# Transposes on TensorE read through fp32r tiles, in a four-stage transformer kernel

## The chip, the cores and the metric

The kernel runs on one core of a Trainium2 chip. The metric is device time in microseconds (us) of one execution; it was run three times. The parts of a core that matter here are TensorE (PE in the profile; its weight loads are listed apart as PEld), VectorE (DVE), ScalarE (ACT), GpSimd (POOL) and SyncE (SP), which issues most of the DMAs. Each engine works its own list of instructions in order and waits on semaphores for the others.

## The reference

Four layers with a residual and a layer norm behind each, on x of 4 x 256 rows of 512 float32 values:

```python
x = L0_attn_hidden_size
x = _layernorm(x + _L0_attn_ref(x, ...))   # 32 heads, latent q and kv, softmax over 256 keys
x = _layernorm(x + _L0_ffn_ref(x, ...))    # silu(x gate.T) * (x up.T), then down, inner width 1376
x = _layernorm(x + _L1_attn_ref(x, ...))   # 32 heads, causal within 128 rows
x = _layernorm(x + _L1_ffn_ref(x, ...))    # dense layer plus 8 gated low-rank experts
```

Both attentions are the usual one:

```python
scores = jnp.einsum('bhqd,bhkd->bhqk', q, k) * scale
probs = jax.nn.softmax(scores, axis=-1)
attn = jnp.einsum('bhqk,bhkd->bqhd', probs, v)
```

## The kernel before

**Numbers.** Nearly every product is made of three matmuls in the reduced 32-bit type fp32r: each operand is split into a high and a low part of that type, and `matmul3` (L101 to L103) adds high x high, low x high and high x low in PSUM. The matmuls whose operands are plain float32 are few: clearing two banks at the start (L354, L361), merging two weights per head (L881), the sum of the first attention's output (L972), and all transposes.

**Transposes.** TensorE contracts over the partitions, so what comes out of one step with rows on the partitions has to be turned before it can be contracted over columns. `pe.transpose(out, in_, identity)` turns one block of 128x128: the block is loaded as weights and the identity is streamed through (one LDWEIGHTS and one MATMUL in the profile, operands `g_ident` and the block). The result lies in PSUM; ACT writes its high part and DVE the low part. There are 1008 blocks:

- L916 (`turn` in the first attention): the probabilities `h_pr`, 4 blocks in a row, 128 times (32 heads x 4 batches).
- L2235 (`turn` in the second attention): `c_pr`, 3 blocks in a row, 128 times.
- L2674 (last layer): the normed rows `e_x`, 4 blocks, 8 times; L2695: the weighted experts `e_wh`, one block, 8 times.
- L1125 and L1153 (class `Norm`): 64 blocks of the rows `g_res`; L406: 8 blocks of `p_kvraw`.
- L1012: a single column of 128 maxima (`mag1`), not counted above.

**First attention (about 26 to 355 us).** The loop runs over heads h and, in a head, over four rounds b, one per batch. TensorE's round is: scores of round s+1 (two `matmul3`), then a query or a projection, then `turn` of round s-1, then the values of round s-3 (L930, four matmuls), then in some rounds the merge of the next head's weights (L881). DVE's round is: inverse of the exp sums (L755), maxima (L750), then by round a part of the merge (L726, which waits for L881), query low part (L744) or output low part (L764), then the low part of the turned probabilities (L759). ACT does the exps (L657) and high parts (L651, L663, L668), POOL the division of the probabilities (L604), which waits for L755 and is waited for by `turn`. Each engine's order is fixed in the code.

**Second attention (about 520 to 1325 us).** A planner lists pieces of PE work of 16 head pairs in one order: scores, turn, values, and between them the projections of the next pair (`c_bx`, `c_by`, `c_bv`). Scores of a step are followed at once by `turn` of an earlier step (L2235).

**Names.** `Kit.sb` reserves a tile and keeps it; `Kit.under` reserves a tile and gives its place back at once, so the next tile reserved has the same addresses. `ident` is made on POOL in `constants` (L263 to L266); `g["ident"]` is what all transposes stream.

Of the kernel before, what the change touches and what calls it, by code (L numbers as in the profile page):

```python
# [34 lines left out]
ALU = mybir.AluOpType  # L35
# [34 lines left out]
    return ap.bitcast(F32)  # L70


def need(eng, sem, value):

    if isinstance(value, int) and value <= 0:
        return
    eng.wait_ge(sem, value)
# [28 lines left out]
class Kit:  # L106
# [5 lines left out]
    def sb(self, name, shape, dt=F32):  # L112
        return self.ctx.enter_context(self.nc.sbuf_tensor(f"{self.tag}_{name}", shape, dt))

    def under(self, name, shape, dt=F32):

        with self.nc.sbuf_tensor(f"{self.tag}_{name}", shape, dt) as tile:
            return tile
# [8 lines left out]
def build(nc, io):  # L127
    with ExitStack() as ctx:
        k = Kit(nc, ctx, "g")
        g = {  # L130
            "res": k.sb("res", [P, NT, HID]),
            "bvs": k.sb("bvs", [P, 1]),
            "xT": (k.sb("xT_hi", [P, KC, T], F32R), k.sb("xT_lo", [P, KC, T], F32R)),
            "ident": k.sb("ident", [P, P]),
            "o_last": k.under("o_last", [P, 2, T], F32R),
            "y": k.sb("y", [P, 4, HID]),
            "wo": k.sb("wo", [P, HID]),
            "mag": k.sb("mag", [P, NH]),
            "mag1": k.sb("mag1", [P, 1]),
            "largest": k.sb("largest", [1, 1], I32),  # L140
            "tick": k.sem("tick"),
            "ln": {n: k.sem(n) for n in ("st", "mv", "add", "rs", "xn", "t", "hi", "lo")},
            "m": {"st": k.sb("st", [P, NT, 6]), "mv": k.sb("mv", [P, NT, 2]), "rs": k.sb("rs", [P, NT]),
                  "mh": k.sb("mh", [P, 4])},
        }
# [56 lines left out]
class Latents0:  # L202
# [7 lines left out]
    def __init__(self, k, io, g, first, down):  # L210
        self.io, self.g, self.first = io, g, first
        self.whi, self.wlo = down
        self.qa = (k.sb("qa_hi", [P, T], F32R), k.sb("qa_lo", [P, T], F32R))
        self.qb = k.sb("qb", [P, T], F32R)
        self.cs = k.sb("cs", [P, NT, P], F32R)
        k.sb("gap0", [P, 16])
        self.kv = (k.sb("kv_hi", [P, T], F32R), k.sb("kv_lo", [P, T], F32R))
        self.bias = k.sb("bias", [P, 16])[:, 0:3]
        self.bv = k.sb("bv", [P, NH])
        self.bo = k.sb("bo", [P, HID])  # L220

        with ExitStack() as ctx:
            t = Kit(k.nc, ctx, "p")
            self.xraw = t.sb("xraw", [P, KC, T])
            self.wraw = t.sb("wraw", [P, KC, 3 * P])
            t.sb("gap", [P, KC, 3 * P])
            self.zero = t.sb("zero", [P, P])
            self.kvraw = t.sb("kvraw", [P, T])
# [29 lines left out]
        sp.wait_ge(self.s_xlo, 2 * KC)  # L258

    def constants(self, pool):  # L260
        ident = self.g["ident"]
        pool.memset(self.zero[:, :], 0.0).then_inc(self.s_id, 1)
        pool.memset(ident[:, :], 0.0).then_inc(self.s_id, 1)  # L263
        pool.wait_ge(self.s_id, 2)
        pool.affine_select(out=ident[:, :], in_=ident[:, :], compare_op=ALU.not_equal, fill=1.0, base=0,
                           pattern=[[-1, P]], channel_multiplier=1).then_inc(self.s_id, 1)  # L266
        pool.memset(self.g["m"]["mh"][:, :], -0.5).then_inc(self.s_pre, 1)
        pool.wait_ge(self.s_xlo, 2 * KC)

# [127 lines left out]
            self.product(pe, i, c)  # L397

    def turn(self, pe, n):
        pe.wait_ge(self.s_id, 3)  # L400
        pe.wait_ge(self.s_raw, n + 1)
        if n:
            pe.wait_ge(self.s_lo, 5)
        for j in range(4):
            a = (4 * n + j) * P
            mm = pe.transpose(self.turn_banks[n][:, j * P:(j + 1) * P], self.kvraw[:, a:a + P], self.g["ident"][:, :])  # L406
        mm.then_inc(self.s_tr, 1)


def attention0_heads(nc, k, io, g, lat, acc, first, tail, norm, ffn, after, attn1, layer1):  # L410
# [13 lines left out]
    with ExitStack() as ctx:  # L424
# [10 lines left out]
        o = [(t.sb(f"o{i}_hi", [P, HALF], F32R), t.sb(f"o{i}_mix", [P, HALF], F32R)) for i in range(2)]  # L435

        gb = t.sb("gb", [P, 16])[:, 0:1]
        pr = [t.sb(f"pr{i}", [P, 2, S]) for i in range(NB)]
        pt = [(t.sb(f"pt{i}_hi", [P, 2, S], F32R), t.sb(f"pt{i}_lo", [P, 2, S], F32R)) for i in range(NB)]
        nmax = [t.sb(f"nmax{i}", [P, 2]) for i in range(NB)]  # L440
        rsum = [t.sb(f"rsum{i}", [P, 2]) for i in range(NB)]
# [83 lines left out]
        with nc.Block() as block:  # L525
# [197 lines left out]
            def _(dve):  # L723
# [44 lines left out]
                def round_(h, b):  # L768
# [22 lines left out]
                        probs(s - 2, (b - 2) % 4)  # L791
                    if isinstance(s, int) and s == NS - 1:
                        dve.wait_ge(s_mag, NH)
                        dve.tensor_reduce(g["mag1"][:, :], g["mag"][:, :], AX, ALU.max).then_inc(s_mag1, 1)
# [79 lines left out]
            def _(pe):  # L874
# [132 lines left out]
                def last_values(d):  # L1007
                    if d == 0:
                        values(NS - 3, NPAIR - 2, 1, 1)
                        pe.wait_ge(s_exp, NS - 1)  # L1010
                        pe.wait_ge(s_mag1, 1)
                        pe.transpose(bs[0][0:1, 0:P], g["mag1"][:, :], ident[:, :]).then_inc(s_magT, 1)  # L1012
                        turn(NS - 1, 3)
                        out(1)
                    elif d == 1:
# [52 lines left out]
class Norm:  # L1068
# [3 lines left out]

    def __init__(self, g, nth):
        self.res, self.xT, self.ident, self.m, self.s = g["res"], g["xT"], g["ident"], g["m"], g["ln"]
        self.tiles = nth * NT
        self.counts = ((1, 2, 3, 3), (4, 4, 6, 8), (9, 9, 10, 10))[nth]

# [42 lines left out]
    def turn(self, pe, j, banks):  # L1120
        pe.wait_ge(self.s["xn"], self.tiles + j + 1)
        need(pe, self.s["lo"], self.tiles + j + 1 - len(banks))
        for c in range(KC):
            cols = slice(c * P, (c + 1) * P)
            i = pe.transpose(banks[j % len(banks)][:, cols], self.res[:, j, cols], self.ident[:, :])  # L1125
        i.then_inc(self.s["t"], 1)

    def view(self, j, banks):
# [17 lines left out]
    def turn_pair(self, pe, a, banks):  # L1146

        pe.wait_ge(self.s["xn"], self.tiles + a + 2)
        for k_half, bank in enumerate(banks):
            for c in range(2):  # L1150
                for i in range(2):
                    k = (2 * k_half + c) * P
                    m = pe.transpose(bank[:, c * S + i * P:c * S + (i + 1) * P], self.res[:, a + i, k:k + P],  # L1153
                                     self.ident[:, :])
            m.then_inc(self.s["t"], 1)

    def view_pair(self, bank):
# [372 lines left out]
class Attention1:  # L1530
# [128 lines left out]
    def programs(self, k, before, after, ffn0, end):  # L1659
# [14 lines left out]
        oT_all = k.sb("oT", [P, 2, 2, T], F32R)  # L1674
        oT = (oT_all[:, 0, :, :], oT_all[:, 1, :, :])

        pr = [k.sb(f"pr{i}", [P, 3 * P]) for i in range(2)]
# [467 lines left out]
        def tensor(pe):  # L2145
# [245 lines left out]
class FFN1:  # L2391
# [4 lines left out]
    def __init__(self, k, io, g, raw, norm):  # L2396
        res, ident, m = g["res"], g["ident"], g["m"]
        ws = [ffn1_part(raw, c)[1:] for c in range(KC)]
        bm = ffn1_part(raw, KC)[1:]
        x = [k.sb(f"x{i}", [P, HID]) for i in range(2)]  # L2400
# [4 lines left out]
        wh = k.sb("wh", [P, E, R])  # L2405
# [264 lines left out]
        def turn(pe, t, u):  # L2670
            pe.wait_ge(s_x, t + 1)
            need(pe, s_xlo, t)
            for c in range(KC):
                i = pe.transpose(bx[:, c * P:(c + 1) * P], x[u][:, c * P:(c + 1) * P], ident[:, :])  # L2674
            i.then_inc(s_tx, 1)

        def first(pe):
# [4 lines left out]
        def tensor(pe):  # L2682
# [9 lines left out]
            def turn_weighted(t):  # L2692
                pe.wait_ge(s_wh, 2 * t + 2)
                need(pe, s_whl, t)
                pe.transpose(bw[:, 0:P], wh[:, :, :].rearrange("p e r -> p (e r)"), ident[:, :]).then_inc(s_tw, 1)  # L2695

            def combined_last():
                out, hi, lo = br[1][:, :], whT[0][:, :], whT[1][:, :]
# [122 lines left out]
```

## Time and profile before

| | |
|---|---|
| median of 3 runs | 1427.53 us (1427.49 to 1427.69) |
| profiled execution, its own time | 1427.42 us |
| span of the profiled execution | 1425.5 us |
| PE busy | 1412.4 us (99%) |
| PEld busy | 1251.5 us (88%) |
| DVE, ACT, POOL busy | 1018.5, 890.7, 773.3 us |
| chain that ended last | PE 94% of the span |

The span runs from the first to the last instruction; 1.9 us of the execution's own time lie around it. "Busy" counts a matmul from its start to its modelled end, and matmuls overlap: what a matmul costs is read from the distance between the starts of neighbours, not from its duration. The profile writes f32 for float32 and for fp32r reads of TensorE alike; which one it is stands in the code.

### The profile page before, as it was taken

To read this page: it belongs to the slowest core of one execution; us is meant where nothing else is said; L and a number is where in the kernel's file an instruction comes from. 1 tells how busy PE (TensorE), PEld (TensorE's weight loads), DVE (VectorE), ACT (ScalarE), POOL (GpSimd) and SP (SyncE) were. 2 spreads that over 40 slices of the span, in tenths; PEclk is the share of its full clock that TensorE was granted. 3 is DMA by queue.
4 is the path that set the end of the run, shared out by engine and by line. 5 is a ranking of instruction groups with operands and counts; after the bars stand their busy time and mean duration, and the time that the engine had idled before them with its cause. 6 is when DMAs were issued, how large, how long until landed. Compare 5 with 4: busy or idle time off the path is not lost.

```text
span 1425.5 us, 30206 instructions
## 1 busy us (share of the span) xinstructions
PE 1412.4 (99%) x8769; PEld 1251.5 (88%) x8769; DVE 1018.5 (71%) x2528; ACT 890.7 (62%) x2445; POOL 773.3 (54%) x827
## 2 busy tenths in 40 slices
PE   9999999999999999999999999999999999999998
PEld 7899999998788888889889889889889889889887
DVE  5999999998868875665665665565565665665776
ACT  5888888888555576555555555556556556556711
POOL 3555555555040367765765665665665665665521
PEclk9999999999999999999999999999999999999999
DMA  5533333322445301111001001001101001000201
GB/s 195 167 95 94 95 94 95 93 66 50 127 140 161 98 30 60 31 30 59 29 29 59 29 29 59 29 29 59 29 29 59 29 29 59 29 29 29 82 16 46
DMA packets 56155, 92.60 MB, mean 65 GB/s; under 512 B 6064, under 2 KB 27312, under 8 KB 56112
## 3 DMA queue, kind: packets, MB, share of 16 engines
q1 hardware_dynamic: 55968, 91.93, 21.5%
q8 instruction: 23, 0.38, 0.1%
q14 instruction: 20, 0.16, 0.0%
q10 hardware_dynamic: 144, 0.13, 0.0%
HBM read 81.82 MB, written 2.10 MB: 59 GB/s over the span
## 4 chain that ended last, share of the span: by engine, by line
PE 94%; DVE 2%; ACT 1%; issue 1%; POOL 1%; DMA 0%; SPq 0%; POOLq 0%; DVEq 0%; ACTq 0%
PE c_bv L101 7%; PE c_bv L102 7%; PE c_bv L103 7%; PE c_bx L101 4%; PE c_bx L103 4%; PE c_bx L102 4%; PE h_bo L930 4%; PE h_bt L916 4%; PE c_by L103 4%; PE c_by L102 4%; PE c_by L101 4%; PE c_bt L2235 3%; PE a_acc L1432 3%; PE h_bo L1432 3%; PE h_bs L101 2%; PE h_bs L103 2%
## 5 line engine op out<-in xcount | busy, mean ns | idle before, releaser
L604 POOL TENSOR_TENSOR h_pr<-h_pr,h_rinv 128x512 f32<-128x512 f32 x128 | 133.2, 1041 | 138.3 <-DVE h_rinv L755 136.0
L1763 POOL TENSOR_TENSOR c_qk<-g_y,c_qk 128x512 fp32r<-128x512 f32 x96 | 124.1, 1293 | 154.1 <-ACT c_qk L1875 147.4
L1614 POOL TENSOR_TENSOR b_sw_lo<-b_slots,b_sw_hi 128x512 fp32r<-128x512 f32 (+1 forms) x128 | 148.1, 1157 | 10.2
L1612 POOL CAST b_sw_hi<-b_slots 128x512 fp32r<-128x512 f32 (+1 forms) x128 | 72.8, 569 | 142.8 <-DMA b_slots<-in_w_qk 123.1
L102 PE MATMUL c_bv<-b_wv_lo,g_xT_hi 128*128 128x256 f32 x496 | 138.8, 280 | 0.0
L101 PE MATMUL c_bv<-b_wv_hi,g_xT_hi 128*128 128x256 f32 x496 | 138.7, 280 | 0.0
L103 PE MATMUL c_bv<-b_wv_hi,g_xT_lo 128*128 128x256 f32 x496 | 138.6, 279 | 0.0
L1984 DVE TENSOR_TENSOR c_bo<-c_bo,g_wo 128x128 f32<-128x128 f32 x128 | 38.3, 299 | 122.6 <-ACT g_wo L1850 118.3
L1875 ACT ACTIVATE c_qk<-g_y 128x512 fp32r<-128x512 f32 x96 | 60.6, 632 | 99.4 <-DVE g_y L2021 69.3
L657 ACT ACTIVATE h_pr<-h_bs,h_nmax 128x256 f32<-128x256 f32 x256 | 119.0, 478 | 2.5 <-DVE h_nmax L750 2.4
L1840 ACT ACTIVATE c_pr<-c_pr,c_rinv 128x128 f32<-128x128 f32 (+1 forms) x256 | 101.9, 448 | 9.0 <-DVE c_rinv L1974 9.0
L102 PEld LDWEIGHTS c_bv<-b_wv_lo,g_xT_hi 128*128 128x128 f32 x496 | 93.1, 188 | 4.5
L101 PEld LDWEIGHTS c_bv<-b_wv_hi,g_xT_hi 128*128 128x128 f32 x496 | 93.2, 188 | 4.4
L1832 ACT ACTIVATE c_pr<-g_wo,c_nmax 128x128 f32<-128x128 f32 x128 | 51.6, 403 | 69.9 <-DVE c_nmax L1970 66.1
L1594 POOL TENSOR_TENSOR b_slots<-b_slots 128x256 f32<-128x256 f32 x128 | 93.1, 747 | 2.5
L1845 ACT ACTIVATE c_pt<-c_bt 128x384 fp32r<-128x384 f32 x128 | 62.9, 491 | 49.5 <-PE c_bt L2235 47.6
L103 PEld LDWEIGHTS c_bv<-b_wv_hi,g_xT_lo 128*128 128x128 f32 x496 | 93.0, 187 | 0.0
L2002 DVE TENSOR_TENSOR g_res<-c_bv,g_res 128x512 f32<-128x512 f32 x103 | 71.2, 691 | 27.4 <-PE c_bv L103 27.3
L750 DVE TENSOR_REDUCE h_nmax<-h_bs 128x2 f32<-128x512 f32 x128 | 87.5, 683 | 0.0
L759 DVE TENSOR_TENSOR h_pt_lo<-h_bt,h_pt_hi 128x512 fp32r<-128x512 f32 x128 | 87.1, 681 | 0.2
L1850 ACT ACTIVATE g_wo<-c_bo 128x128 f32<-128x128 f32 x128 | 35.4, 276 | 78.5 <-PE c_bo L2247 78.5
L101 PE MATMUL c_bv<-b_wo_hi,c_oT 128*128 128x512 f32 x200 | 82.0, 410 | 0.0
(479 smaller groups left out, 5184.0 us busy)
## 6 DMA issues: line engine op xcount, KB each, us to landing
f_wi<-in_w_ffn SPq DMA_DIRECT2D x66, 256.0 KB, 2.7
b_slots<-in_w_qk SPq DMA_DIRECT2D x64, 256.0 KB, 2.9
a_w<-in_w_head SPq DMA_DIRECT2D x28, 352.0 KB, 2.9
h_part<-in_w_ffn SPq DMA_DIRECT2D x32, 264.0 KB, 2.7
b_raw_v<-in_w_v SPq DMA_DIRECT2D x16, 512.0 KB, 4.5
b_raw_o<-in_w_o SPq DMA_DIRECT2D x16, 512.0 KB, 4.6
h_o_mix<-h_o_hi SPq DMA_DIRECT2D x62, 128.0 KB, 2.2
b_ffn_w<-in_w_ffn SPq DMA_DIRECT2D x4, 576.0 KB, 5.5
```

Of the source, the lines that this page charges most:

```text
L101: pe.matmul(out, w[0], x[0], start=start, stop=False, skip_group_check=True)
L102: pe.matmul(out, w[0], x[1], start=False, stop=False, skip_group_check=True)
L103: return pe.matmul(out, w[1], x[0], start=False, stop=stop, skip_group_check=True)
L604: pool.tensor_tensor(pr[b][:, :, :], pr[b][:, :, :], rinv[b][:, :][:, :, None].to_broadcast([P, 2, S]), ALU.mult)\
L657: m = act.activation(pr[b][:, i, :], bs[b % 2][:, i * S:(i + 1) * S], ACT.Exp, bias=nmax[b][:, i:i + 1], accum_out=rsum[b][:, i:i + 1])
L750: dve.tensor_reduce(nmax[b][:, :], bs[b % 2][:, :].rearrange("p (a n) -> p a n", a=2), AX, ALU.max, negate=True).then_inc(s_max, 1)
L759: dve.tensor_tensor(pt[b][1][:, :, :], bt[b % 2][:, :].rearrange("p (a n) -> p a n", a=2), f32(pt[b][0][:, :, :]), ALU.subtract).then_inc( ...
L1432: m = pe.matmul(out, a, b, start=start and i == 0, stop=stop and i == len(pairs) - 1, skip_group_check=True)
L1594: pool.tensor_tensor(slot(out), slot(a), slot(b), op).then_inc(self.s_comb, 1)
L1614: pool.tensor_tensor(self.sw[1][:, a:b], self.slots[:, a:b], f32(self.sw[0][:, a:b]), ALU.subtract)\
L1763: pool.tensor_tensor(lo, src, f32(hi), ALU.subtract).then_inc(s_sumlo, 1)
L1840: m = act.activation(x[:, cols], x[:, cols], ACT.Identity, scale=rinv[t % 2][:, i:i + 1])
```

## The change

All transposes go through a new helper, and what they read is declared fp32r. A matmul operand's type is that of its tile, so each tile that is turned gets a twin of type fp32r at the same addresses (`turned`): the twin is reserved and given back, and the float32 tile takes its place. The writers of the tile still write float32; `transpose` reads the twin, and its output in PSUM is seen as fp32r. The identity is a tile of type fp32r: POOL makes it in a float32 tile `square` as before and then copies it (one instruction more); the first transposes wait for the fourth increment instead of the third. On PE, DVE, ACT and SP the instructions and their order are the same as before; POOL has the one copy more, at the start.

```diff
+def transpose(pe, out, rows, ident):
+    return pe.transpose(out.bitcast(F32R), rows, ident)
...
+    def turned(self, name, shape):
+        return self.under(name + "_t", shape, F32R), self.sb(name, shape)
...
-            "ident": k.sb("ident", [P, P]),
+            "ident": k.sb("ident", [P, P], F32R),
...
-        pool.memset(ident[:, :], 0.0).then_inc(self.s_id, 1)
+        pool.memset(square[:, :], 0.0).then_inc(self.s_id, 1)
         pool.wait_ge(self.s_id, 2)
-        pool.affine_select(out=ident[:, :], in_=ident[:, :], compare_op=ALU.not_equal, fill=1.0, base=0,
+        pool.affine_select(out=square[:, :], in_=square[:, :], compare_op=ALU.not_equal, fill=1.0, base=0,
                            pattern=[[-1, P]], channel_multiplier=1).then_inc(self.s_id, 1)
+        pool.wait_ge(self.s_id, 3)
+        pool.tensor_copy(self.g["ident"][:, :], square[:, :]).then_inc(self.s_id, 1)
...
-        pe.wait_ge(self.s_id, 3)
+        pe.wait_ge(self.s_id, 4)
...
-        pr = [t.sb(f"pr{i}", [P, 2, S]) for i in range(NB)]
+        pr_t, pr = zip(*(t.turned(f"pr{i}", [P, 2, S]) for i in range(NB)))
...
-                            m = pe.transpose(bt[b % 2][:, kt * S + i * P:kt * S + (i + 1) * P],
-                                             pr[b][:, i, kt * P:(kt + 1) * P], ident[:, :])
+                            m = transpose(pe, bt[b % 2][:, kt * S + i * P:kt * S + (i + 1) * P],
+                                          pr_t[b][:, i, kt * P:(kt + 1) * P], ident[:, :])
...
-                    m = pe.transpose(bt[:, cols], pr[t % 2][:, cols], ident[:, :])
+                    m = transpose(pe, bt[:, cols], pr_t[t % 2][:, cols], ident[:, :])
```

The other calls (L406, L1012, L1125, L1153, L2674, L2695) are changed in the same way.

## Rows read from the trace of the kernel before

**Rows 1.** The page: busy time and instructions; granted TensorE clock in 40 slices.
```profile
PE 1412.4 (99%) x8769; PEld 1251.5 (88%) x8769; DVE 1018.5 (71%) x2528; ACT 890.7 (62%) x2445; POOL 773.3 (54%) x827
...
PEclk9999999999999999999999999999999999999999
```

**Rows 2.** Stretches: length, busy PE, PEld, DVE, ACT, POOL, granted clock, DMA, GB/s.
```profile
60.00:340.00 280.00, 279.61 (x2024) 255.57 (x2024) 261.56 (x576) 232.22 (x685) 151.08 (x195) 1.00 0.33 89
340.00:370.00 30.00, 28.78 (x172) 21.56 (x171) 26.93 (x58) 18.36 (x47) 9.54 (x13) 1.00 0.14 40
...
489.00:520.00 31.00, 30.46 (x187) 26.02 (x186) 27.06 (x54) 17.90 (x30) 14.79 (x17) 1.00 0.01 1
520.00:1000.00 480.00, 478.92 (x2974) 428.87 (x2974) 293.96 (x828) 286.93 (x822) 306.18 (x311) 1.00 0.13 42
```

**Rows 3.** Waits, 60 to 340 us: who for whom, us in total, times, longest.
```profile
DVE h_gm L726 <- PE h_bq L881: 10.7, 25, 0.4
...
PE h_bt L916 <- POOL h_pr L604: 0.4, 2, 0.2
```

**Rows 4.** Groups by shape, PE: busy us, mean ns of one, idle before.
```profile
L916 PE MATMUL h_bt<-g_ident,h_pr 128*128 128x128 f32 x512 | 77.2, 273 | 1.3 <-POOL h_pr L604 1.3
...
L2235 PE MATMUL c_bt<-g_ident,c_pr 128*128 128x128 f32 x384 | 63.0, 273 | 0.4 <-ACT c_pr L1840 0.2
```

**Rows 5.** Groups by shape, weight loads.
```profile
L101 PEld LDWEIGHTS c_bv<-b_wv_hi,g_xT_hi 128*128 128x128 f32 x496 | 93.2, 188 | 4.4
L916 PEld LDWEIGHTS h_bt<-g_ident,h_pr 128*128 128x128 f32 x512 | 60.5, 140 | 16.7 <-issue 4.7 <-POOL h_pr L604 2.7
...
L881 PEld LDWEIGHTS h_bq<-a_w 128*128 128x128 f32 x112 | 14.9, 190 | 0.1
```

**Rows 6.** Timeline, PE, second attention: start, length of the piece, instructions.
```profile
604.15 0.22 PE L2247 MATMUL c_bo<-c_pt,c_v_lo 128*128 128x128 f32 x1
604.21 0.33 PE L2225 MATMUL c_bs<-c_qk 128*128 128x256 f32 x1
...
604.85 0.49 PE L2235 MATMUL c_bt<-g_ident,c_pr 128*128 128x128 f32 x3
...
605.41 0.39 PE L102 MATMUL c_bx<-b_ts,b_sw_hi 128*128 128x512 f32 x1
605.64 0.40 PE L103 MATMUL c_bx<-b_ts,b_sw_lo 128*128 128x512 f32 x1
```

**Rows 7.** Timeline, weight loads, three short windows in the first attention.
```profile
351.74 0.14 PEld L916 LDWEIGHTS h_bt<-g_ident,h_pr 128*128 128x128 f32 x1 [0.94 <-POOL h_pr L604]
...
351.74 0.20 PEld L916 LDWEIGHTS h_bt<-g_ident,h_pr 128*128 128x128 f32 x2 [0.94 <-POOL h_pr L604]
...
153.06 0.19 PEld L930 LDWEIGHTS h_bo<-h_pt_hi,a_cs 128*128 128x128 f32 x1
153.16 0.19 PEld L930 LDWEIGHTS h_bo<-h_pt_lo,a_cs 128*128 128x128 f32 x1
```

**Rows 8.** Timeline, PE: float32 matmuls of 512 columns, one and two.
```profile
352.23 0.59 PE L972 MATMUL a_acc<-g_wo,z_os 128*128 128x512 f32 x1
...
352.23 1.02 PE L972 MATMUL a_acc<-g_wo,z_os 128*128 128x512 f32 x2
```

**Rows 9.** Timeline, one head of the first attention: DVE, POOL, PE.
```profile
152.08 0.29 DVE L726 TENSOR_SCALAR h_gm<-h_bq 128x128 f32<-128x128 f32 x1 [0.43 <-PE h_bq L881]
...
162.29 0.29 DVE L726 TENSOR_SCALAR h_gm<-h_bq 128x128 f32<-128x128 f32 x1 [0.43 <-PE h_bq L881]
...
159.53 1.04 POOL L604 TENSOR_TENSOR h_pr<-h_pr,h_rinv 128x512 f32<-128x512 f32 x1 [0.40 <-DVE h_rinv L755]
...
160.78 0.60 PE L916 MATMUL h_bt<-g_ident,h_pr 128*128 128x128 f32 x4
...
161.34 0.28 PE L930 MATMUL h_bo<-h_pt_lo,a_cs 128*128 128x256 f32 x1
161.46 0.28 PE L930 MATMUL h_bo<-h_pt_hi,a_cs 128*128 128x256 f32 x1
```

More of the change, by code:

```diff
@@ L129, in build @@
         k = Kit(nc, ctx, "g")
+        res_t, res = k.turned("res", [P, NT, HID])
         g = {
-            "res": k.sb("res", [P, NT, HID]),
+            "res": res, "res_t": res_t,
             "bvs": k.sb("bvs", [P, 1]),
             "xT": (k.sb("xT_hi", [P, KC, T], F32R), k.sb("xT_lo", [P, KC, T], F32R)),
-            "ident": k.sb("ident", [P, P]),
+            "ident": k.sb("ident", [P, P], F32R),
             "o_last": k.under("o_last", [P, 2, T], F32R),
@@ L138, in build @@
             "mag": k.sb("mag", [P, NH]),
-            "mag1": k.sb("mag1", [P, 1]),
+            "mag1": k.turned("mag1", [P, 1]),
             "largest": k.sb("largest", [1, 1], I32),
@@ L225, in __init__ @@
             self.wraw = t.sb("wraw", [P, KC, 3 * P])
-            t.sb("gap", [P, KC, 3 * P])
+            self.square = t.sb("square", [P, P])
+            t.sb("gap", [P, (3 * KC - 1) * P])
             self.zero = t.sb("zero", [P, P])
-            self.kvraw = t.sb("kvraw", [P, T])
+            self.kvraw_t, self.kvraw = t.turned("kvraw", [P, T])
         self.s_x, self.s_res, self.s_bv, self.s_pre = (k.sem(n) for n in ("x_in", "res_in", "bv_in", "pre"))
@@ L260, in constants @@
     def constants(self, pool):
-        ident = self.g["ident"]
+        square = self.square
         pool.memset(self.zero[:, :], 0.0).then_inc(self.s_id, 1)
-        pool.memset(ident[:, :], 0.0).then_inc(self.s_id, 1)
+        pool.memset(square[:, :], 0.0).then_inc(self.s_id, 1)
         pool.wait_ge(self.s_id, 2)
-        pool.affine_select(out=ident[:, :], in_=ident[:, :], compare_op=ALU.not_equal, fill=1.0, base=0,
+        pool.affine_select(out=square[:, :], in_=square[:, :], compare_op=ALU.not_equal, fill=1.0, base=0,
                            pattern=[[-1, P]], channel_multiplier=1).then_inc(self.s_id, 1)
+        pool.wait_ge(self.s_id, 3)
+        pool.tensor_copy(self.g["ident"][:, :], square[:, :]).then_inc(self.s_id, 1)
         pool.memset(self.g["m"]["mh"][:, :], -0.5).then_inc(self.s_pre, 1)
@@ L405, in turn @@
             a = (4 * n + j) * P
-            mm = pe.transpose(self.turn_banks[n][:, j * P:(j + 1) * P], self.kvraw[:, a:a + P], self.g["ident"][:, :])
+            mm = transpose(pe, self.turn_banks[n][:, j * P:(j + 1) * P], self.kvraw_t[:, a:a + P],
+                           self.g["ident"][:, :])
         mm.then_inc(self.s_tr, 1)
@@ L793, in round_ @@
                         dve.wait_ge(s_mag, NH)
-                        dve.tensor_reduce(g["mag1"][:, :], g["mag"][:, :], AX, ALU.max).then_inc(s_mag1, 1)
+                        dve.tensor_reduce(g["mag1"][1][:, :], g["mag"][:, :], AX, ALU.max).then_inc(s_mag1, 1)
                     if asked and c == 0:
@@ L1011, in last_values @@
                         pe.wait_ge(s_mag1, 1)
-                        pe.transpose(bs[0][0:1, 0:P], g["mag1"][:, :], ident[:, :]).then_inc(s_magT, 1)
+                        transpose(pe, bs[0][0:1, 0:P], g["mag1"][0][:, :], ident[:, :]).then_inc(s_magT, 1)
                         turn(NS - 1, 3)
@@ L1074, in __init__ @@
         self.res, self.xT, self.ident, self.m, self.s = g["res"], g["xT"], g["ident"], g["m"], g["ln"]
+        self.res_t = g["res_t"]
         self.tiles = nth * NT
@@ L1124, in turn @@
             cols = slice(c * P, (c + 1) * P)
-            i = pe.transpose(banks[j % len(banks)][:, cols], self.res[:, j, cols], self.ident[:, :])
+            i = transpose(pe, banks[j % len(banks)][:, cols], self.res_t[:, j, cols], self.ident[:, :])
         i.then_inc(self.s["t"], 1)
@@ L1152, in turn_pair @@
                     k = (2 * k_half + c) * P
-                    m = pe.transpose(bank[:, c * S + i * P:c * S + (i + 1) * P], self.res[:, a + i, k:k + P],
-                                     self.ident[:, :])
+                    m = transpose(pe, bank[:, c * S + i * P:c * S + (i + 1) * P], self.res_t[:, a + i, k:k + P],
+                                  self.ident[:, :])
             m.then_inc(self.s["t"], 1)
@@ L1675, in programs @@
         oT = (oT_all[:, 0, :, :], oT_all[:, 1, :, :])
-        pr = [k.sb(f"pr{i}", [P, 3 * P]) for i in range(2)]
+        pr_t, pr = zip(*(k.turned(f"pr{i}", [P, 3 * P]) for i in range(2)))
         rinv = [k.sb(f"rinv{i}", [P, 2]) for i in range(2)]
@@ L2399, in __init__ @@
         bm = ffn1_part(raw, KC)[1:]
-        x = [k.sb(f"x{i}", [P, HID]) for i in range(2)]
+        x_t, x = zip(*(k.turned(f"x{i}", [P, HID]) for i in range(2)))
         xb = [k.sb(f"xb{i}", [P, HID]) for i in range(2)]
@@ L2404, in __init__ @@
         prod = k.sb("prod", [P, E * DK])
-        wh = k.sb("wh", [P, E, R])
+        wh_t, wh = k.turned("wh", [P, E, R])
         whT = (k.sb("whT_hi", [P, P], F32R), k.sb("whT_lo", [P, P], F32R))
@@ L2673, in turn @@
             for c in range(KC):
-                i = pe.transpose(bx[:, c * P:(c + 1) * P], x[u][:, c * P:(c + 1) * P], ident[:, :])
+                i = transpose(pe, bx[:, c * P:(c + 1) * P], x_t[u][:, c * P:(c + 1) * P], ident[:, :])
             i.then_inc(s_tx, 1)
@@ L2694, in turn_weighted @@
                 need(pe, s_whl, t)
-                pe.transpose(bw[:, 0:P], wh[:, :, :].rearrange("p e r -> p (e r)"), ident[:, :]).then_inc(s_tw, 1)
+                transpose(pe, bw[:, 0:P], wh_t[:, :, :].rearrange("p e r -> p (e r)"), ident[:, :]).then_inc(s_tw, 1)
             def combined_last():
```

## The prediction

> **What bounds the kernel now.** I read the page first: TensorE is busy 99% of the span, its granted clock stands in the top tenth in all forty slices [rows 1]. So the time is TensorE's list, as long as nothing else is late. Then the table by stretches, to see where that is true. In the second attention DVE is busy 294 of 480 us, ACT 287, POOL 306: every other engine has a third of its time free, and PE is at 479 [rows 2]. In the first attention DVE is busy 262 of 280 us; PE is still at 280, but DVE is just behind it. So a nanosecond saved on PE is worth a nanosecond in the second attention, and in the first only until DVE is the bound. The waits of the first attention say how far that is: DVE waits once per head, 25 times in the stretch, 10.7 us in total, 0.43 us each, for the merge matmuls L881; PE waits 0.4 us in all for POOL [rows 3]. Between two heads lie 162.29 - 152.08 = 10.21 us [rows 9]. DVE therefore has 9.78 us of its own per head.
>
> **What one transpose costs now.** Durations mislead, since matmuls overlap; starts count. In the second attention the three transposes start at 604.85 and the second 512-column matmul behind them at 605.41, which is 0.56 us for three transposes and one such matmul; the next distance, 605.41 to 605.64, is 0.23 for one alone [rows 6]. So three cost 0.33, or 0.11 each. In the first attention, 160.78 to 161.34 is 0.56 for four transposes and one matmul of 256 columns, which alone takes 161.46 - 161.34 = 0.12: again 0.11 each [rows 9].
>
> Two things could set this 0.11. One is streaming: the float32 matmuls L972 with 512 columns start 1.02 - 0.59 = 0.43 us apart [rows 8], fp32r ones of 512 columns 0.23 apart [rows 6]. A float32 operand streams at half the pace, and 128 float32 columns are then 0.43 / 4 = 0.11. The other is the weight load. An ordinary load (L930, fp32r) is followed by the next after 153.16 - 153.06 = 0.10 to 0.11 us. A transpose's load that stands free (PE had waited 0.94 us) is followed by the next after 0.20 - 0.14 = 0.06 us [rows 7]; it is also shorter on average, 140 ns against 188 of the fp32r matmuls and 190 of the float32 ones at L881 [rows 5]. So in a transpose of today the streaming (0.11) is the slow half and the load (0.06) the fast one.
>
> **The change part by part.** The identity becomes fp32r, and fp32r streams 128 columns in 604.21 - 604.15 = 0.06 us [rows 6]. If the load keeps its 0.06, a transpose that is followed by another costs 0.06 instead of 0.11: 0.05 saved. The last of a group saves nothing: the matmul behind it needs an ordinary load of 0.10 to 0.11, which today is hidden behind the last transpose's 0.11 of streaming and would then stick out by what the streaming lost. So a group of n saves (n - 1) x 0.05. The unknown is the load under the new type, since no fp32r transpose runs before: from below 0.06 (today's transposes), from above 0.11 (today's fp32r loads of ordinary matmuls, in which case the load alone sets 0.11 and nothing is saved). I take 0.06, because ordinary loads are equally long for float32 and fp32r, 190 and 188 ns, and only the transposes' are short at 140 [rows 5]: the rows point to the transposing and not to the type. Both ends are kept for the range.
>
> The Trainium skill ("TensorE: Matmul & The Clock Gate", section "LDWEIGHTS (loading the stationary operand)") speaks against the change: a load takes the number of columns over 1.2 GHz, 107 ns for 128, whatever is loaded. The free-standing load of today's transposes, 0.06 apart [rows 7], does not agree with it, the ordinary loads do; by the rule alone the sum below would be zero.
>
> - Second attention, 384 transposes [rows 4] in 128 groups of three: 128 x 2 x 0.05 = 12.8 us. All on the path, by [rows 2]. Bounds 0 and 14.
> - First attention, 512 transposes [rows 4] in 128 groups of four: PE's list shrinks by 128 x 3 x 0.05 = 19.2 us, 0.60 per head, to 9.61 us. That is less than DVE's own 9.78, so the whole of it can't come. What DVE waits for is L881, which stands behind the transposes of the same round. Those become 0.15 shorter. They can also start a little earlier: POOL has finished their input at 159.53 + 1.04 = 160.57, PE comes to them at 160.78 [rows 9]; PE will be early after the change and needs the load of 0.06 and the signal from POOL. Without any time for the signal it would start at 160.63, which is 0.15 earlier; with a slow one, nothing is gained. I take the middle, 0.08. DVE's wait falls by 0.15 + 0.08 = 0.23 per head and 0.20 stay. What is late next is POOL's division, and behind it DVE's own order; PE gets idle time of about 0.60 - 0.23 = 0.37 us per head before L916. Over 32 heads: 7.4 us. Bounds: 0.15 x 32 = 4.8 when PE can't start earlier; 0.43 x 32 = 13.8 when the whole wait goes.
> - Last layer, 32 transposes (the kernel's text has their number) in 8 groups of four: 8 x 3 x 0.05 = 1.2 us. The single blocks (L2695) save nothing.
> - The norms' 64 and the 8 of the first keys: 18 groups of four, of which many stand in pairs, so about 60 x 0.05 = 3.0 us of PE. They lie in stretches where DVE is busy 27 of 30 and 27 of 31 us [rows 2]; I count half, 1.5.
> - POOL's copy of the identity is one instruction in the first three microseconds; the first transposes come after 15 us. Nothing, and at most its own some tenths if POOL's list there were late.
> - ACT and DVE read the same PSUM bytes with the same instructions: nothing.
>
> Sum: 12.8 + 7.4 + 1.2 + 1.5 = 22.9 us. The profiled execution took 1427.42 us (span 1425.5 and 1.9 around it), 0.1 below the median of the runs. 1427.4 - 22.9 = 1404.5; I say 1404.
>
> **The rivals.**
> 1. *The new type brings the ordinary load.* The transposes' load becomes 0.11 (or the streaming stays at half pace because all 32 bits have to pass, which comes to the same). For it: every fp32r matmul in the trace has a load of 0.10 to 0.11; that the page's rule says so too is told above. Against it: the short load of today's transposes is of float32, whose ordinary load is as long as fp32r's [rows 5]. Time: 1427.5, within 0.2%.
> 2. *The first attention gives nothing.* The pace is 0.06, but DVE's wait only moves: what PE no longer spends on L916 it spends waiting for POOL, and DVE waits on something else in its round. For it: DVE is busy 93% there [rows 2]. Against it: L881 is directly behind the shortened group. Time: 1427.4 - 15.5 = 1412.
> 3. *Slower: an ordinary load in front of an unchanged stream.* Loads of 0.11 while the streaming stays 0.11. Within a group the two overlap, but the first load of a group that comes late, right after its wait, is not covered, and it is 0.05 longer than today. This decides where PE comes to a group with less than 0.11 of streaming before it: if in all 128 groups of the first attention, 6.4 us, 1434 us. Against it: matmuls of 256 or 512 columns (0.12 and 0.23) stand in front of the groups and would hide it.
>
> **How the numbers follow.** The forecast has 0.54, rival 1 0.26, rival 2 0.12, rival 3 0.08. The forecast's own range is 1396 (12.8 + 13.8 + 1.2 + 3.0 = 30.8 less) to 1409 (4.8 in the first attention). About 0.2% is what a measurement of this kernel can tell from no change, here 2.9 us. Faster: 0.54 + 0.12 = 0.66. Rival 1 is the same: 0.26. Slower: 0.08. To hold eight in ten the range must reach rival 1: 1396 to 1429.
>
> **What the profile would show.** In the timeline of the second attention, the start of the three transposes to the start of the second matmul behind them falls from 0.56 to about 0.46; transposes start 0.06 apart. The mean of an L2235 or L916 matmul falls by some 0.05 from 273 ns, that of the loads stays near 140 ns. If the loads show 188 ns, rival 1 is right. In the first attention heads come every 9.98 us, L726 waits 0.20, and PE shows waits for L604 of up to 0.37 us per head; with 0.43 still at L726, rival 2. The forecast is wrong if the group in the second attention still takes 0.56, or if its stretch does not shrink by 12 to 13 us.

## The result, and the profile after

The changed kernel takes 1416.95 us (median of 4 runs, 1415.87 to 1417.77), the kernel before beside it 1427.51 (1426.71 to 1427.69). The ratio is 0.9927 with a 95% interval of 0.9909 to 0.9944: it is faster, by 10.6 us where 22.9 had been worked out. The time lies inside the range of 1396 to 1429, but outside the forecast's own of 1396 to 1409, and the forecast of 1404 does not stand.

The page after, its first lines (busy us and instructions of each engine), against [rows 1]:

```profile
span 1414.1 us, 30207 instructions
...
PE 1400.2 (99%) x8769; PEld 1236.6 (87%) x8769; DVE 1017.3 (72%) x2528; ACT 891.2 (63%) x2445; POOL 774.0 (55%) x828
```

PE is busy 12.2 us less, and still 99%. The groups by shape, which answer to [rows 4, 5] (all transposes now have the helper's line L75, and `h_pr_t` and `c_pr_t` are the twins; L101 to L103 are L106 to L108 here, the values L930 are L944, the merge L881 is L895, DVE's L726 and L755 are L740 and L769, POOL's L604 is L618, and some experiments move them by up to 3 more):

```profile
L75 PE MATMUL h_bt<-g_ident,h_pr_t 128*128 128x128 f32 x512 | 61.3, 242 | 1.6 <-POOL h_pr L618 1.6
...
L75 PE MATMUL c_bt<-g_ident,c_pr_t 128*128 128x128 f32 x384 | 48.3, 235 | 0.4 <-ACT c_pr L1855 0.2
...
L75 PEld LDWEIGHTS h_bt<-g_ident,h_pr_t 128*128 128x128 f32 x512 | 54.9, 141 | 20.2 <-issue 7.8 <-POOL h_pr L618 3.2
```

A transpose's matmul is 31 to 38 ns shorter, not 50. The load's duration is what it was, 141 ns against 140; by my own test ("if the loads show 188 ns, rival 1 is right") rival 1 is out, and the forecast looks right. It is not, as the starts show. The timeline of PE in the second attention, against [rows 6]:

```profile
766.31 0.38 PE L75 MATMUL c_bt<-g_ident,c_pr_t 128*128 128x128 f32 x3
766.52 0.46 PE L106 MATMUL c_bx<-g_xT_hi,b_sw_hi 128*128 128x512 f32 x1
766.82 0.39 PE L107 MATMUL c_bx<-g_xT_lo,b_sw_hi 128*128 128x512 f32 x1
767.05 0.39 PE L108 MATMUL c_bx<-g_xT_hi,b_sw_lo 128*128 128x512 f32 x1
```

From the group to the second matmul behind it are 766.82 - 766.31 = 0.51 us, 0.56 before and 0.46 forecast; less the 0.23 of one matmul, three transposes cost 0.28 instead of 0.33. The free-standing loads, against [rows 7], one and two of them:

```profile
139.07 0.14 PEld L75 LDWEIGHTS h_bt<-g_ident,h_pr_t 128*128 128x128 f32 x1 [0.31 <-issue]
...
139.07 0.23 PEld L75 LDWEIGHTS h_bt<-g_ident,h_pr_t 128*128 128x128 f32 x2 [0.31 <-issue]
```

The next load starts 0.23 - 0.14 = 0.09 us after the first, where it was 0.06 in float32. That is the number the forecast lacked.

Where the time came from is read by the start of the same matmul in both traces. The second attention's first and last groups, before and after:

```profile
520.19 0.55 PE L2235 MATMUL c_bt<-g_ident,c_pr 128*128 128x128 f32 x3
...
1347.75 0.51 PE L2235 MATMUL c_bt<-g_ident,c_pr 128*128 128x128 f32 x3
```
```profile
515.50 0.45 PE L75 MATMUL c_bt<-g_ident,c_pr_t 128*128 128x128 f32 x3
...
1337.16 0.41 PE L75 MATMUL c_bt<-g_ident,c_pr_t 128*128 128x128 f32 x3
```

The table has the start of the very first transpose of each kind and of the very last one, which is the last of its group:

| matmul | before | after | gained so far |
|---|---|---|---|
| first transpose of h_pr | 29.83 | 29.26 | 0.6 |
| last transpose of h_pr | 354.92 | 351.44 | 3.5 |
| first transpose of c_pr | 520.19 | 515.50 | 4.7 |
| last transpose of c_pr | 1347.99 | 1337.32 | 10.7 |
| end of the span | 1425.5 | 1414.1 | 11.4 |

So the first attention gives 2.9 us (7.4 forecast), the second 6.0 (12.8), the first layers' start, norms and feed-forward 0.6 + 1.2 (1.5), the last layer 0.7 (1.2). The 0.6 at the start can't be told from chance: in the eight versions of the changed kernel without trial instructions the first transpose of h_pr comes anywhere from 28.6 to 30.2 us. And the execution in the trace is the fastest of the four (1415.87 us), so the 11.4 of the table are 0.8 more than the 10.6 of the medians.

One head of the first attention, POOL and PE, against [rows 9]:

```profile
158.17 1.04 POOL L618 TENSOR_TENSOR h_pr<-h_pr,h_rinv 128x512 f32<-128x512 f32 x1 [0.40 <-DVE h_rinv L769]
```
```profile
159.35 0.54 PE L75 MATMUL h_bt<-g_ident,h_pr_t 128*128 128x128 f32 x4
159.72 0.36 PE L944 MATMUL h_bo<-h_pt_hi,a_cs 128*128 128x256 f32 x1
159.91 0.28 PE L944 MATMUL h_bo<-h_pt_lo,a_cs 128*128 128x256 f32 x1
```

and DVE at the merge, two heads, with its waits from 60 to 340 us, against [rows 9, 3]:

```profile
160.86 0.29 DVE L740 TENSOR_SCALAR h_gm<-h_bq 128x128 f32<-128x128 f32 x1 [0.43 <-PE h_bq L895]
...
170.99 0.29 DVE L740 TENSOR_SCALAR h_gm<-h_bq 128x128 f32<-128x128 f32 x1 [0.43 <-PE h_bq L895]
```
```profile
DVE h_gm L740 <- PE h_bq L895: 10.2, 24, 0.4
...
PEld h_bt L75 <- issue: 7.1, 23, 0.3
```

PE comes to the last group 159.35 - 159.21 = 0.14 us after POOL's end, 0.21 before: it starts 0.07 earlier relative to its input, as forecast (0.08). But from its start to the second L944 are still 0.56 us, and DVE's wait for the merge is still 0.43. A head takes 10.13 instead of 10.21.

### The profile page after: what moved, and what is told of

It is laid out like the page before. It is cut to its first block, busy times and chain, and to the rows that moved or that the text cites. A ratio compares the mean times of both kernels' runs of the same rounds, so it can differ in the third digit from the quotient of the medians.

```text
span 1414.1 us, 30207 instructions
## 1 busy us (share of the span) xinstructions
PE 1400.2 (99%) x8769; PEld 1236.6 (87%) x8769; DVE 1017.3 (72%) x2528; ACT 891.2 (63%) x2445; POOL 774.0 (55%) x828
## 4 chain that ended last, share of the span: by engine, by line
PE 94%; DVE 2%; ACT 1%; issue 1%; POOL 1%; DMA 1%; SPq 0%; POOLq 0%; DVEq 0%; ACTq 0%
PE c_bv L106 8%; PE c_bv L108 7%; PE c_bv L107 7%; PE c_bx L106 5%; PE h_bo L944 5%; PE c_bx L108 4%; PE c_bx L107 4%; PE c_by L106 4%; PE c_by L108 4%; PE c_by L107 4%; PE h_bo L1447 3%; PE a_acc L1447 3%; PE h_bt L75 3%; PE h_bs L106 2%; PE c_bt L75 2%; PE h_bs L108 2%
## 5 line engine op out<-in xcount | busy, mean ns | idle before, releaser
L618 POOL TENSOR_TENSOR h_pr<-h_pr,h_rinv 128x512 f32<-128x512 f32 x128 | 133.2, 1041 | 136.7 <-DVE h_rinv L769 134.3
L1629 POOL TENSOR_TENSOR b_sw_lo<-b_slots,b_sw_hi 128x512 fp32r<-128x512 f32 (+1 forms) x128 | 148.1, 1157 | 10.2
L106 PE MATMUL c_bv<-b_wv_hi,g_xT_hi 128*128 128x256 f32 x496 | 138.8, 280 | 0.2 <-DVE g_xT_lo L1183 0.2
L108 PE MATMUL c_bv<-b_wv_hi,g_xT_lo 128*128 128x256 f32 x496 | 138.8, 280 | 0.0
L106 PEld LDWEIGHTS c_bv<-b_wv_hi,g_xT_hi 128*128 128x128 f32 x496 | 93.0, 187 | 4.7 <-DVE g_xT_lo L1183 0.3
L108 PEld LDWEIGHTS c_bv<-b_wv_hi,g_xT_lo 128*128 128x128 f32 x496 | 93.1, 188 | 0.0
L764 DVE TENSOR_REDUCE h_nmax<-h_bs 128x2 f32<-128x512 f32 x128 | 87.5, 684 | 0.0
L106 PE MATMUL c_bv<-b_wo_hi,c_oT 128*128 128x512 f32 x200 | 81.4, 407 | 0.0
```

What stands on the lines that cost most here:

```text
L106: pe.matmul(out, w[0], x[0], start=start, stop=False, skip_group_check=True)
L108: return pe.matmul(out, w[1], x[0], start=False, stop=stop, skip_group_check=True)
L618: pool.tensor_tensor(pr[b][:, :, :], pr[b][:, :, :], rinv[b][:, :][:, :, None].to_broadcast([P, 2, S]), ALU.mult)\
L764: dve.tensor_reduce(nmax[b][:, :], bs[b % 2][:, :].rearrange("p (a n) -> p a n", a=2), AX, ALU.max, negate=True).then_inc(s_max, 1)
L1629: pool.tensor_tensor(self.sw[1][:, a:b], self.slots[:, a:b], f32(self.sw[0][:, a:b]), ALU.subtract)\
```

## The experiments

All edits are to the changed kernel unless said.

**1 and 2. Each attention back to float32.**

```diff
-    m = transpose(pe, bt[...], pr_t[b][:, i, ...], ident[:, :])
+    m = pe.transpose(bt[...], pr[b][:, i, ...], f32(ident[:, :]))
```

undo_first: 

> The changed kernel with the first attention's transposes (h_pr) read as float32 again, all others as fp32r. Theory A (each transpose of a group costs 0.085 us instead of 0.11, and the first attention could take only 0.07 us per head of it because of a chain over POOL and DVE): the first attention goes back to 10.21 us per head and the run is about 3 us slower than the changed kernel, near 1420; the second attention keeps its gain of 5.7 us. Theory B (the saved time of the first attention shows up in later stages, because TensorE comes to them earlier): the loss is larger, 5 us or more.

undo_second: 

> The changed kernel with the second attention's transposes (c_pr) read as float32 again, all others as fp32r. Theory A: 128 groups lose 0.044 us each, 5.7 us; near 1422.6, and the distance from a group's start to the second matmul behind it is 0.56 us again. Theory B (the second attention's gain is a matter of other waits, not of the group's own length): a loss other than 5 to 6 us.

Measured: 1419.94 us, ratio 0.9951 (0.9937 to 0.9964), and 1423.11, 0.9972 (0.9961 to 0.9982): 3.0 and 6.2 us more than the changed kernel. In the first one's trace the first c_pr transpose comes at 518.50 (3.0 late) and the last at 1340.42 (3.1 late). In the second one's they come at 516.73 and 1344.62, 827.9 us apart as in the kernel before (827.8; changed 821.8), and the distance from a group's start to the second matmul behind it is 0.56 us again. So each attention's gain arises in its own stretch. Theory A holds.

**3 and 4. POOL's value weights before the division of round 3,** in the changed kernel and in the one before.

```diff
                     s = 4 * h + b
+                    if b == 3 and has(h - 1, TAIL0):
+                        split_wv(h - 1)
                     if has(s - 1, NS) and not (isinstance(s, int) and s == 1):
                         scaled(s - 1, (b - 1) % 4)
...
-                    if b == 3 and has(h - 1, TAIL0):
-                        split_wv(h - 1)
```

after_pool: 

> The changed kernel, and in the first attention POOL splits the value weights before the division of round 3 instead of behind it. Theory A (a chain DVE L769, POOL division, value weights, loop end, POOL division, last group of transposes, merge, DVE L740 sets the head's length in the changed kernel): the division before the last group starts 0.2 to 0.3 us earlier, DVE's wait for the merge falls from 0.43 to about 0.2 us, a head takes 9.9 instead of 10.13 us; 5 to 7 us less than the changed kernel, 1410 to 1412. Theory B (PE's own list sets the head's length): no difference, 1417.

before_pool: 

> The kernel before with the same move on POOL. Theory A: here PE is at the group 0.09 us after POOL could let it, so little can be gained before PE's own list (10.2 us per head) binds: 0 to 2 us less than the kernel before, 1425.5 to 1427.5. Theory B: no difference. If it gains as much as in the changed kernel, the chain and not the transposes was the bound of both.

Measured: 1415.04 us, 0.9914 (0.9901 to 0.9928), and 1427.59, 1.0002 (0.9993 to 1.0011). In the loop the head's length falls from 10.13 to 10.02 us in the changed kernel and stays 10.20 in the one before. So the chain over POOL hides part of the transposes' gain, and only once they are faster: with the move in both, the transposes give 0.18 us per head instead of 0.08. The move does the same to POOL in both: the division before the last group starts 0.08 us after its input from DVE (L769, L755) has ended, where it was 0.34 in the changed kernel and 0.28 in the one before. But in the kernel before PE doesn't come earlier for it; it starts the group 0.40 us after POOL's end instead of 0.20, so there PE's own list holds the head. The size was over-estimated: 1.9 us less than the changed kernel where 5 to 7 were expected, 10.02 us per head instead of 9.9, and DVE's wait fell to 0.30, not 0.2. The first heads, written out before the loop, lose a little: from the first group of transposes to the ninth are 21.2 us where they were 20.8 (the whole run's start differs by more, as said under the result).

**5. The instructions by themselves.** Sixteen of a kind in a row at the program's start, into a PSUM bank that is cleared afterwards, with 512-column matmuls between:

```diff
+                mr(40, 512)
+                tf(16)        # float32 transposes
+                mr(4, 512)
+                tr(16)        # fp32r transposes
+                mr(4, 512)
+                tr(16, 64)    # 64 columns of weights
...
                 lat.clear(pe, acc)
```

> The changed kernel with a row of trial instructions on TensorE before its first own ones; they write a PSUM bank that is cleared afterwards, and only the distances between their starts are read. Behind each stretch stand four 512-column matmuls. Sixteen each of: float32 transposes of 128x128; fp32r ones; fp32r and float32 ones of 64 columns (half the weights, 128 columns streamed); fp32r ones of 64 rows (128 columns of weights, 64 streamed); ordinary fp32r matmuls with new weights and 128 or 64 columns streamed; then single and double transposes between 512- and 256-column matmuls. Theory L (under fp32r the transpose's weight load itself takes 0.085 us and is proportional to the columns loaded): 0.11, 0.085, about 0.06 for 64 columns of weights, 0.085 for 64 rows, 0.11 for the ordinary ones. Theory S (the load takes 0.057 as under float32, but can't start until 0.028 us after the stream before it has begun): 0.11, 0.085, 0.085 for 64 columns of weights, and about 0.06 for 64 rows.

The timeline of PE, three of the stretches (start, length from the first start to the last end, count):

```profile
31.75 1.12 PE L75 MATMUL h_bs<-g_ident 128*64 128x128 f32 x16
...
33.69 1.91 PE L1059 MATMUL h_bs<-g_ident,p_zero 128*64 128x128 f32 x16
...
36.45 1.51 PE L75 MATMUL h_bs<-g_ident 64*128 64x64 f32 x16
```

L75 is fp32r, L1059 float32; "128*64" is rows x columns of the weights. The float32 stretches turn a block of zeros, the fp32r ones the identity. With the last one's own 0.22 to 0.27 us taken off and divided by 15: fp32r with half the weights 0.060, float32 with half the weights 0.109, fp32r with half the rows (and so half the streaming) 0.084. In the same trace the full fp32r block runs at 0.087 (median; the first few are shorter) and the ordinary fp32r matmuls of 128 and 64 columns at 0.111 and 0.112. Halving what is streamed changes nothing, halving what is loaded does: theory L, the load is the bound, and theory S falls. With 64 columns of weights the fp32r stream of 128 columns takes no more than the 0.060.

The same run has pairs of transposes, each pair followed by one 512-column matmul, six times in fp32r and six in float32:

```profile
47.81 0.29 PE L75 MATMUL h_bs<-g_ident 128*128 128x128 f32 x2
...
49.95 0.28 PE L75 MATMUL h_bs<-g_ident 128*128 128x128 f32 x2
...
50.37 0.38 PE L1059 MATMUL h_bs<-g_ident,p_zero 128*128 128x128 f32 x2
...
52.64 0.38 PE L1059 MATMUL h_bs<-g_ident,p_zero 128*128 128x128 f32 x2
```

A round takes (49.95 - 47.81) / 5 = 0.43 us in fp32r and (52.64 - 50.37) / 5 = 0.45 in float32: two transposes save one step of 0.025, and the last of a group saves nothing.

**6. Is it the type that makes the load longer?**

```diff
+                for rows, a in ((P, P), (64, P), (32, P), (32, 64), (32, 32)):
+                    for t in (tf, tr):
+                        t(16, rows, a)
+                        mr(4, 512)
```

> As the first trial row, with other shapes: sixteen transposes each of 128x128, 64 rows x 128 columns, 32 x 128, 32 x 64 and 32 x 32, in float32 and in fp32r. The rows set the columns streamed, the columns the weights loaded. The question is whether the fp32r type made the load longer or whether the load always took 0.085 us and stood behind the float32 stream. Theory T (the load depends on the type, 0.06 in float32 and 0.085 in fp32r): 64 rows in float32 start 0.06 apart, in fp32r 0.085. Theory U (the load is the same): float32 with 64 or 32 rows also starts 0.085 apart, since its stream is then shorter than the load. With fewer columns of weights both go below 0.06 in both theories.

The weight loads of the two stretches with 64 rows, float32 (L1059) and fp32r (L75):

```profile
30.81 1.08 PEld L1059 LDWEIGHTS h_bs<-g_ident,p_zero 64*128 64x128 f32 x16 [0.37 <-issue]
...
33.09 1.40 PEld L75 LDWEIGHTS h_bs<-g_ident 64*128 64x128 f32 x16 [0.36 <-issue]
```

With 0.14 for the last: (1.08 - 0.14) / 15 = 0.063 us from load to load in float32, (1.40 - 0.14) / 15 = 0.084 in fp32r. With 32 rows, before the clock changed, it is the same, (1.07 - 0.14) / 15 = 0.062 and (1.40 - 0.14) / 15 = 0.084:

```profile
35.65 1.07 PEld L1059 LDWEIGHTS h_bs<-g_ident,p_zero 32*128 32x128 f32 x16 [0.36 <-issue]
...
37.89 1.40 PEld L75 LDWEIGHTS h_bs<-g_ident 32*128 32x128 f32 x16 [0.36 <-issue]
```

Theory T: the transpose's load depends on the type. The type of the block, of the identity and of the output changed together, and which of them does it was not tried; the free-standing loads of real probabilities, 0.06 and 0.09 above, speak against the zeros as the cause. An ordinary load doesn't depend on it: the float32 matmuls of the merge in the kernel before have (0.53 - 0.19) / 3 = 0.11 us from load to load, like the fp32r ones of [rows 7].

```profile
161.58 0.53 PEld L881 LDWEIGHTS h_bq<-a_w 128*128 128x128 f32 x4
```

The float32 load of 0.06 that the prediction read off [rows 7] is right for float32; it does not carry over. The shapes of 32 x 64 and 32 x 32 are not read, since the clock changed there (last section).

**7. More transposes.** Every block of the second attention turned twice.

```diff
-                    m = transpose(pe, bt[:, cols], pr_t[t % 2][:, cols], ident[:, :])
+                    for _ in range(2):
+                        m = transpose(pe, bt[:, cols], pr_t[t % 2][:, cols], ident[:, :])
```

> The changed kernel with every block of the second attention turned twice (384 transposes more, groups of six). Theory A: 0.085 us each, 32.6 us more, 1449.5. My prediction's size of 0.06 would give 23 us, 1440; no gain inside a group would give 42 us, 1459.

Measured: 1446.77 us, 1.0137 (1.0121 to 1.0152), 29.8 us more for 384 transposes, 0.078 each. A group in the middle of the stretch:

```profile
898.54 0.63 PE L75 MATMUL c_bt<-g_ident,c_pr_t 128*128 128x128 f32 x6
899.01 0.46 PE L106 MATMUL c_bv<-b_wo_hi,c_oT 128*128 128x512 f32 x1
899.32 0.40 PE L107 MATMUL c_bv<-b_wo_lo,c_oT 128*128 128x512 f32 x1
```

The median distance from a group's start to the second matmul behind it grows from 515 to 764 ns, 0.083 per transpose. The run shows 2.8 us less than the 32.6 expected: from the 17th group to the 121st each added transpose costs 0.084, in the first sixteen and the last seven groups less. The forecast's 0.06 (23 us) and no gain (42 us) are both out.

**8 and 9. Which groups of the first attention give the gain.**

```diff
-                            m = transpose(...)
+                            to = bt[b % 2][:, kt * S + i * P:kt * S + (i + 1) * P]
+                            if b in (1, 2):      # only_03: (0, 3)
+                                m = transpose(pe, to, pr_t[b][:, i, kt * P:(kt + 1) * P], ident[:, :])
+                            else:
+                                m = pe.transpose(to, pr[b][:, i, kt * P:(kt + 1) * P], f32(ident[:, :]))
```

only_12: 

> The changed kernel, but in the first attention only the transposes of the batches 1 and 2 are read as fp32r; those of 0 and 3 are float32 again. Theory A (the group of batch 0 gives its gain to a wait for DVE's output low part L778 behind it, that of batch 3 is paced by POOL and its first load is uncovered): nothing is lost against the changed kernel, 10.13 us per head, 1417. Theory B (every group gives the same quarter): half of the first attention's 3 us is lost, 1418.5.

only_03: 

> The changed kernel, but in the first attention only the transposes of the batches 0 and 3 are read as fp32r; those of 1 and 2 are float32 again. Theory A: the whole gain of the first attention is lost, 10.2 us per head, 1420, as with all four undone. Theory B: 1418.5.

Measured: 1419.14 us, 0.9943 (0.993 to 0.9957), and 1417.62, 0.9933 (0.992 to 0.9947). The intervals overlap, the traces don't: a head takes 10.20 us with batches 1 and 2 alone and 10.14 with 0 and 3 alone. Theory A as written falls, and with the signs turned round: the groups that I had called worthless give all, the others almost nothing. The last group (batch 3) in the two traces, only_12 first:

```profile
140.30 0.65 PE L934 MATMUL h_bt<-g_ident,h_pr 128*128 128x128 f32 x4
140.71 0.36 PE L947 MATMUL h_bo<-h_pt_hi,a_cs 128*128 128x256 f32 x1
140.92 0.28 PE L947 MATMUL h_bo<-h_pt_lo,a_cs 128*128 128x256 f32 x1
```
```profile
138.68 0.46 PE L75 MATMUL h_bt<-g_ident,h_pr_t 128*128 128x128 f32 x4
138.98 0.35 PE L947 MATMUL h_bo<-h_pt_hi,a_cs 128*128 128x256 f32 x1
139.17 0.28 PE L947 MATMUL h_bo<-h_pt_lo,a_cs 128*128 128x256 f32 x1
```

With 1 and 2 alone PE is early, and the float32 group takes 140.92 - 140.30 = 0.62 us to the second L947. With 0 and 3 alone PE is not early, the group's first load starts 0.08 us before its matmul, under the 512-column matmul before it (0.01 in the changed kernel), and the group takes 139.17 - 138.68 = 0.49 us. Over 17 heads of each trace (from about 119 to 284 us), medians in ns and the head's length in us:

| | POOL's end to PE's start | start to 2nd L930 (L944, L947) | sum | head |
|---|---|---|---|---|
| before | 204 | 561 | 763 | 10.21 |
| changed | 134 | 567 | 701 | 10.13 |
| only 1, 2 | 133 | 612 | 745 | 10.20 |
| only 0, 3 | 208 | 485 | 696 | 10.14 |
| first attention undone | 200 | 557 | 759 | 10.21 |

The head's length follows the sum: 0.062 less and 0.075 less, 0.018 and 0.009, 0.067 and 0.072. Being early lengthens the group by 0.05 us in float32 (561 to 612) and by 0.08 in fp32r (485 to 567), about one load of its type. From POOL's end to the values behind the last group is the piece of the chain that the change can shorten. Either PE comes early and its first load is then uncovered, or it comes at the old time and the group is shorter; it gets about 0.07 us once, not twice. The group of batch 0 indeed gives its gain to the wait for DVE: the load behind it comes 0.19 us after the last transpose's start, 0.09 before, and in both traces 0.05 after the end of DVE's L778 (L764). Batches 0 and 3 were not changed one at a time; that it is batch 3 rests on these distances.

**10. The POOL move inside the loop only.**

```diff
+                    early = b == 3 and not isinstance(h, int)
+                    if early:
+                        split_wv(h - 1)
...
-                    if b == 3 and has(h - 1, TAIL0):
+                    if b == 3 and has(h - 1, TAIL0) and not early:
                         split_wv(h - 1)
```

> The changed kernel with POOL's value weights split before the division of round 3 inside the loop over heads only; in the heads written out before and behind it the old order stays. The first version of this move lost 1.3 us before the loop and won 2.7 us in it. If the loss came from the heads written out, this one keeps the 10.02 us per head and is 1 us below it, 1414; if it came from somewhere else, 1415 again.

Measured: 1414.31 us (1413.38 to 1414.97), 0.9906 (0.989 to 0.9923). A head takes 10.02 us and the early heads no longer lose: from the first group to the ninth are 20.6 us. The 1.3 us of the expectation were misread, since 0.9 of them lay before the first group, in the part where runs differ anyway; the loss of the first version in the written heads was 0.4. It is the fastest version here; its interval overlaps that of the changed kernel, the ranges of the runs don't. DVE at the merge and POOL around it:

```profile
149.76 0.29 DVE L743 TENSOR_SCALAR h_gm<-h_bq 128x128 f32<-128x128 f32 x1 [0.30 <-PE h_bq L898]
...
159.79 0.29 DVE L743 TENSOR_SCALAR h_gm<-h_bq 128x128 f32<-128x128 f32 x1 [0.32 <-PE h_bq L898]
```
```profile
154.46 0.46 POOL L612 TENSOR_TENSOR h_wv_both<-a_wv,h_wv_both 64x128 fp32r<-64x128 f32 x1
155.08 1.04 POOL L618 TENSOR_TENSOR h_pr<-h_pr,h_rinv 128x512 f32<-128x512 f32 x1 [0.16 <-POOL h_wv_both L612]
156.95 1.04 POOL L618 TENSOR_TENSOR h_pr<-h_pr,h_rinv 128x512 f32<-128x512 f32 x1 [0.83 <-DVE h_rinv L772]
```

The last of these is the division before the last group, and it now waits for DVE alone. DVE's reciprocal in front of it, in this run and, for the 158.17 shown above, in the changed kernel:

```profile
156.71 0.17 DVE L772 RECIPROCAL h_rinv<-h_rsum 128x2 f32<-128x2 f32 x1
```
```profile
157.66 0.17 DVE L769 RECIPROCAL h_rinv<-h_rsum 128x2 f32<-128x2 f32 x1
```

It starts 156.95 - 156.88 = 0.07 us after its input, where it was 158.17 - 157.83 = 0.34. The groups of batches 1 to 3 are then each 0.07 to 0.08 us shorter than in the kernel before, 0.22 together, of which the head shows 0.19; that of batch 0 still has its wait for DVE.

## Why the prediction was wrong, point by point

- **The bound** was right: PE in the second attention, PE and a chain over DVE and POOL in the first.
- **What one transpose cost** was right: 0.11 us, set by the float32 stream, the load behind it at 0.06 (0.109 and 0.063 in experiments 5 and 6). That the stream would halve was right too.
- **"I take 0.06" for the load under the new type is the step that failed.** It is 0.085, between the two ends that the text named. The argument was that ordinary loads are equally long in both types and so the type would not matter for a transpose's either. It compared durations, which for loads say little of the pace. By starts, too, an ordinary load takes 0.11 in both types, but a transpose's takes 0.063 and 0.085 (experiment 6). A transpose followed by another saves 0.025, not 0.05. For the second attention that is 128 x 2 x 0.025 = 6.4 us against 6.0 measured, where 12.8 stood. The same goes for the last layer and the norms. With 0.025 for 0.05 and all else as it stands the whole sum is 6.4 + 5.0 + 0.6 + 0.7 = 12.7 us instead of 22.9, so this one term is 10.2 of the 12.3 us that are missing.
- **The last of a group saves nothing**: right (the pairs of experiment 5). With 0.025 the groups of three save 0.05 (0.56 to 0.51), those of four 0.07 to 0.08 (0.56 to 0.49) where the first load is covered.
- **The first attention** has most of the other 2.1 us. The half on the start time was right: 0.08 taken, 0.07 measured. The half on the group's length (0.15) came out as nothing, for two reasons that the text missed: the load's size, and that a PE that has to wait for POOL has no matmul in front of the group to hide its first load. The two gains exclude each other (experiments 8 and 9). DVE's wait, which was to fall to 0.20, stayed at 0.43 because DVE too came earlier by the same amount: the 9.78 us that were called DVE's own became 10.13 - 0.43 = 9.70. They were not all its own: by [rows 2] DVE is busy 261.56 / 280 x 10.21 = 9.54 us per head, and the rest is idle time. 2.9 us instead of 7.4.
- **The rivals.** Rival 1 (the ordinary load of 0.11) was half right: the type does lengthen the load, but only to 0.085. The rule of the Trainium skill that it was told with ("TensorE: Matmul & The Clock Gate", section "LDWEIGHTS (loading the stationary operand)": columns over 1.2 GHz, 107 ns for 128) fits the ordinary loads here, 0.11 us from load to load, and no transpose in either type. Rival 2 had the right place, and the sign named for it came (0.43 still at L726). Its 1412 is the nearest of the sums to 1416.95, but by luck: it counts with the 0.06 that is wrong, and with nothing from the first attention, which gave 2.9. Rival 3 did not happen.
- **The range** held the time because it reached to rival 1, not because the forecast's own range (1396 to 1409) did.

## What to carry to other kernels

When the half of an instruction that sets its pace gets faster, the other half can become the bound, and what was read of it while it was hidden belongs to the old form. Here the price of the new form lay between its two nearest relatives, and the forecast had taken the better one. In a chain where one engine waits for another, arriving early and being short can be the same gain: here what hid the first load was the work that the engine no longer had in front of it. And a faster engine can pay more once the order on its supplier is changed too: here the same move on POOL gave nothing before and a tenth of a microsecond per head after.

## What the runs showed of the hardware

- The duration of a weight load doesn't give its pace: a transpose's load has 140 ns and 141 ns in the traces before and after, with 0.063 and 0.085 us from load to load (experiment 6).
- In experiment 6 the granted clock fell while PE was busy without a gap. Stretches of its trace (columns as in [rows 2]):

```profile
20.00:39.00 19.00, 19.00 (x140) 15.75 (x138) 0.00 (x0) 0.00 (x0) 0.00 (x0) 1.00 0.01 2
39.00:39.50 0.50, 0.50 (x6) 0.47 (x6) 0.00 (x0) 0.00 (x0) 0.00 (x0) 0.97 0.00 0
39.50:55.00 15.50, 15.50 (x93) 11.51 (x94) 0.00 (x0) 0.00 (x0) 0.00 (x0) 0.50 0.00 1
```

  From 35.7 us on it ran rows of transposes with 32 rows, four matmuls of 512 columns after each row. The clock was 1.00 (2.4 GHz) from 20 us to 39, through the stretches of 128 and 64 rows and the two with 32 rows and 128 columns (to 39.3), and stood at 0.50 (1.2 GHz) from 39.5 us to 55. With blocks of 128x128, as in the kernel, it stayed at 1.00 ([rows 1] and the page after). Whether the 32 rows are the cause was not tried by itself.
